# One tower layer on one core: GELUs of the second group behind the sines of the first, its last projections between the chunks, means as extra columns

## The reference, cut to what matters

```
h   = silu(layernorm([atom_embed[x], (rel_dist masked @ neighbor_embed[x]) * w_rd] @ w1 + b1)) @ w2 + b2
x1  = layernorm(h)
# attention without a softmax, by phases
content, values, key_ph = x1 @ mc_w, x1 @ ve_w, tanh(x1 @ cpe_w) * PI
ao      = gelu([x1, pp] @ hop_w1 + b) @ hop_w2 + b       # 4 heads x (32 phases + 1 width)
center, width = tanh(ao[:32]) * PI, sigmoid(ao[32]) * 2 + 0.1
gate    = sigmoid(gelu(x1 @ sg_w1 + b) @ sg_w2 + b)
ctx     = cumsum(x1 @ kce_w + b) / pos
st_ph   = tanh(gelu([x1, ctx] @ ksk_w1 + b) @ ksk_w2 + b) * PI
# causal sums over cos/sin of position, centre (5 shifts, weighted), key and stored phases
comb    = mh_out(content, center, width) + kv_ret(values * gate, key_ph, st_ph)
h       = h + x1 + layernorm(comb) @ out_w + out_b
x2      = layernorm(h)
h       = h + sum over the top 2 of 8 experts of (gelu(x2 @ W1[e] + b1[e]) @ W2[e] + b2[e])
```

## Time and profile before

| | |
|---|---|
| median of 3 runs | 169.94 us (169.46 to 170.4) |
| profiled execution, its own time | 169.19 us |
| its span | 167.4 us |
| busy in the span: PE / PEld | 149.0 us / 88.4 us |
| DVE / ACT / POOL | 116.6 / 81.8 / 8.8 us |
| spin products (L590) | 24.5 us of PE |
| ten of them from 58.60 | 2.32 us |
| chain that ended last | PE 54%, DVE 32%, ACT 6%, issue 6% |
| table loads on ACT | 1.28 us each |

### The profile page before, as it was taken

The page is one execution under the profiler, slowest core; times in us unless marked ns, Lnnn a source line. Parts: engine busy times, 40 slices in busy tenths (PEclk is TensorE's granted clock), DMA queues, the critical chain, the costliest instruction groups (busy, mean ns, idle before and its releaser), DMA issues.

```text
span 167.4 us, 2358 instructions
## 1 busy us (share of the span) xinstructions
PE 149.0 (89%) x806; PEld 88.4 (53%) x812; DVE 116.6 (70%) x344; ACT 81.8 (49%) x137; POOL 8.8 (5%) x38
## 2 busy tenths in 40 slices
PE   5899999999999988649699997786999999899991
PEld 1382565537693336429586752463665764553530
DVE  6999879975798989499859899993434788031202
ACT  3001151469389637962970232897224366545721
POOL 5403100140000000000000000000000000000000
PEclk9999999999999999956858999999999999999999
DMA  4899950300000000000000000000000000002011
GB/s 119 321 427 427 417 205 6 125 0 0 0 4 0 0 0 2 0 2 0 0 4 0 0 4 0 0 2 0 0 4 0 0 4 0 0 0 63 0 31 31
DMA packets 3778, 9.21 MB, mean 55 GB/s; under 512 B 2356, under 2 KB 2484, under 8 KB 3256
## 3 DMA queue, kind: packets, MB, share of 16 engines
q1 hardware_dynamic: 3768, 9.08, 14.6%
HBM read 8.55 MB, written 0.52 MB: 54 GB/s over the span
## 4 chain that ended last, share of the span: by engine, by line
PE 54%; DVE 32%; ACT 6%; issue 6%; POOL 0%; DVEq 0%; POOLq 0%; ACTq 0%
PE bank L960 9%; PE bank L944 6%; PE bank L646 5%; PE bank L945 4%; PE bank L624 3%; PE bank L807 2%; DVE invpos L1035 2%; PE bank L637 2%; DVE q_sc L1295 2%; DVE q_sc L1288 2%; PE bank L712 1%; PE bank L812 1%; PE bank L603 1%; PE bank L676 1%; DVE dist_sb L1274 1%
## 5 line engine op out<-in xcount | busy, mean ns | idle before, releaser
L590 PE MATMUL bank<-spin 128*128 128x512 bf16 x92 | 24.5, 398 | 5.2 <-POOL spin L328 2.0
L574 ACT ACTIVATE hid<-bank 128x512 f32<-128x512 f32 x32 | 17.9, 602 | 21.5 <-PE bank L945 21.4
L590 PEld LDWEIGHTS bank<-spin 128*128 128x128 bf16 x98 | 9.2, 104 | 15.8 <-issue 2.7
L960 PE MATMUL bank<-hid,ffn_sb 128*64 128x512 f32 x64 | 16.4, 612 | 0.0
L944 PE MATMUL bank<-xp,w1hi 128*128 128x512 f32 x32 | 14.6, 455 | 0.9 <-ACT xp L554 0.9
L1406 DVE TENSOR_TENSOR h<-bank,h 128x256 f32<-128x256 f32 (+1 forms) x5 | 1.8, 367 | 18.6 <-PE bank L971 12.8
L1313 DVE TENSOR_TENSOR dist_sb<-bank,fold_sb 128x256 f32<-128x256 f32 x16 | 6.0, 419 | 10.4 <-PE bank L812 9.8
L945 PE MATMUL bank<-xp,w1lo 128*128 128x512 f32 x32 | 12.6, 395 | 0.0
L944 PEld LDWEIGHTS bank<-xp,w1hi 128*128 128x128 f32 x32 | 6.0, 188 | 7.9 <-ACT hid L574 3.6
L646 PE MATMUL bank<-dist_sb,neigh 128*64 128x512 f32 x32 | 9.3, 699 | 0.0
L1085 DVE TENSOR_TENSOR dist_sb<-dist_sb,mask_in 128x1024 f32<-128x1024 f32 x8 | 9.2, 1218 | 0.0
(11 more groups left out here) (270 smaller groups left out, 318.3 us busy)
## 6 DMA issues: line engine op xcount, KB each, us to landing
dist_sb<-in_dist SPq DMA_DIRECT2D x4, 1024.0 KB, 11.2
mask_in<-in_mask SPq DMA_DIRECT2D x2, 512.0 KB, 8.1
fold_sb<-in_folded SPq DMA_DIRECT2D x1, 998.0 KB, 11.0
ffn_sb<-in_ffn SPq DMA_DIRECT2D x1, 816.0 KB, 17.4
late_sb<-in_late SPq DMA_DIRECT2D x1, 728.5 KB, 15.9
mask_in<-in_mrows SPq DMA_DIRECT2D x1, 512.0 KB, 3.1
out<-h SPq DMA_DIRECT2D x8, 64.0 KB, 1.7
early_sb<-in_early SPq DMA_DIRECT2D x1, 167.0 KB, 2.4
```

Source lines behind the costliest of these rows:

```text
L574: nc.scalar.activation(hid[:, at % HB], bank[hid_bank[at % 3]][:, :], ACT.Gelu).then_inc(S["hid_set"], 1)
L590: nc.tensor.matmul(bank[i][:, :], spin[:, 0:P], spin[:, :], start=True, stop=True)
L960: mm = nc.tensor.matmul(bank[2][j * D:(j + 1) * D, :], K["e_w2"][:, (e + j) * D:(e + j + 1) * D], hid[:, (at + j) % HB], start=False, stop ...
```

## The change

1. **Means as columns.** `w2_mean` and `out_mean` become the last two columns of `w2_ext` and `outw_ext` [128, 130]. The products write chunks 0, 1 to bank 5 and chunks 2, 3 to bank 7; the separate mean products go; VectorE reads rows and means in two halves.
2. **Position part first.** The product of the position phases opens the hop accumulation, ahead of the wait for x_t, in place of three spins.
3. **GELUs.** For group 1 ScalarE's hop, gate and ksk GELUs are one step, P1(2), which `ORDER` puts behind Q0(6), the first group's sines. For that TensorE makes group 1's storage product (into bank 6) and last joints in P1(2) too, with spins and waits between.
4. **Order.** Group 1's P(3), P(4), P(5) lie between the first group's chunk steps C(2) to C(5); Q1(4), Q1(5) come behind X0(2), and Q1(6) behind X0(4). From C1(1) on the order is the old one.
5. `weight_parts` is moved one step later and its expert half becomes `expert_parts`, after the third mask step. More spins in C0(1), C0(2) and X0(4).

```diff
+        w2_ext = sb("w2_ext", [P, PM])                       # PM = P + NH_
+        w2c_bd, w2_mean = w2_ext[:, 0:P], w2_ext[:, P:PM]
+        outw_ext = sb("outw_ext", [P, PM])
+        ksk_bank = (2, 6)
+        def with_mean(n):
+            return bank[5 + 2 * n][:, 0:2 * PM].rearrange("p (c d) -> p c d", d=PM)
...
@@ ScalarE, project @@
                 nc.scalar.activation(sg_g[:, :], bank[2][0:2 * SGH, :], ACT.Gelu,
                                      bias=K["sg_b1"]).then_inc(S["sg_set"], 1)
-                yield
+                if g == 0:
+                    yield
                 act.wait_ge(S["ksk_mm"], g + 1)
...
+                nc.scalar.activation(ksk_g[:, :], bank[ksk_bank[g]][:, :], ACT.Gelu,
                                      bias=ksk_bias[:, :]).then_inc(S["ksk_set"], 1)
+                if g:
+                    yield
@@ TensorE, token @@
                 for c in range(NC):
-                    mm = nc.tensor.matmul(bank[5][:, c * P:(c + 1) * P], f_t[:, c * P:(c + 1) * P], w2c_bd[:, :],
+                    mm = nc.tensor.matmul(with_mean(c // 2)[:, c % 2], f_t[:, c * P:(c + 1) * P], w2_ext[:, :],
                                           start=True, stop=True)
...
-                    mm = nc.tensor.matmul(bank[7][:, c * NH_:(c + 1) * NH_], f_t[:, c * P:(c + 1) * P], w2_mean[:, :],
-                                          start=True, stop=True)
@@ TensorE, project @@
-                spin_products(3, 2)
+                if g:
+                    pe.wait_ge(S["st_set"], g)
+                nc.tensor.matmul(bank[1][:, :], K["hop1p"], K["pp_T"], start=True, stop=False)
                 pe.wait_ge(S["xt_set"], g + 1)
-                nc.tensor.matmul(bank[1][:, :], K["hop1x_bd"], x_t[:, :], start=True, stop=False)
-                nc.tensor.matmul(bank[1][:, :], K["hop1p"], K["pp_T"], start=False, stop=True).then_inc(S["hop_mm"], 1)
+                nc.tensor.matmul(bank[1][:, :], K["hop1x_bd"], x_t[:, :], start=False, stop=True).then_inc(S["hop_mm"], 1)
...
                 joint(0, 3)
                 joint(1, 0)
-                yield
                 if g:
                     pe.wait_ge(S["h1_norm"], NG)
-                    spin_products(4, 6)
-                    pe.wait_ge(S["k_feat"], 2)
-                    spin_products(6, 6)
-                    pe.wait_ge(S["at_arg"], 1)
-                    spin_products(6, 6)
+                    storage()
+                    pe.wait_ge(S["h_mean_set"], NG)
+                    spin_products(4, 7)
+                    pe.wait_ge(S["phi_set"], 1)
+                    spin_products(5, 7)
+                    pe.wait_ge(S["th_sum"], 2)
+                    spin_products(5, 7)
+                    pe.wait_ge(S["th_set"], 2)
+                    spin_products(3, 7)
+                    last_joints()
+                    spin_products(3, 7)
+                    pe.wait_ge(S["cos_set"], 1)
+                    spin_products(5, 7)
+                    pe.wait_ge(S["cos_set"], 2)
+                    spin_products(5, 7)
+                yield
@@ TensorE, chunks @@
+                if g == 0:
+                    pe.wait_ge(S["h_mean_set"], NG)
+                    spin_products(4, 2)
+                    pe.wait_ge(S["kph_abs_set"], 1)
+                    spin_products(5, 2)
+                    pe.wait_ge(S["k_feat"], 1)
+                    spin_products(5, 2)
...
                 yield
+                if g == 0:
+                    pe.wait_ge(S["ksk_set"], NG)
+                    pe.wait_ge(S["q_cos"], 2)
+                    spin_products(5, 7)
                 pe.wait_ge(S["q_sum"], 2 * g + 2)
@@ TensorE, chunks, step 8 @@
-                    mm = nc.tensor.matmul(bank[5][:, c * P:(c + 1) * P], cc_t[:, c * P:(c + 1) * P], outw_g[:, :],
+                    mm = nc.tensor.matmul(with_mean(c // 2)[:, c % 2], cc_t[:, c * P:(c + 1) * P], outw_ext[:, :],
                                           start=True, stop=True)
-                    mm = nc.tensor.matmul(bank[7][:, c * NH_:(c + 1) * NH_], cc_t[:, c * P:(c + 1) * P], out_mean[:, :],
@@ TensorE, experts, step 4 @@
                     spin_products(6, 2)
+                    pe.wait_ge(S["at_arg"], 2)
+                    spin_products(5, 2)
+                    pe.wait_ge(S["phi_set"], 2)
+                    spin_products(5, 2)
+                    pe.wait_ge(S["th_sum"], 4)
+                    spin_products(5, 2)
                     pe.wait_ge(S["first_best"], 1)
@@ VectorE, chunks, step 9 @@
-                link(nc.vector.tensor_tensor(v8(comb[:]), b3(5), bc(st_c[:, :], D), ALU.mult))
+                for n in range(2):
+                    dve.wait_ge(S["attn_mm"], 2 * g + n + 1)
+                    factor = st_c[:, 4 * n:4 * n + 4].rearrange("p (c f) -> p c f", f=NH_).unsqueeze(3).broadcast_to([P, 2, NH_, D])
+                    ins = nc.vector.tensor_tensor(comb[:, 2 * n:2 * n + 2], rows_of(n), factor, ALU.mult)
```

More of the change, by code:

```diff
@@ L284, in b3, with rows_of, means_of @@
             return bank[i][:, :].rearrange("p (t d) -> p t d", d=D)
+        def with_mean(n):
+            return bank[5 + 2 * n][:, 0:2 * PM].rearrange("p (c d) -> p c d", d=PM)
+        def rows_of(n):
+            return with_mean(n)[:, :, 0:P].rearrange("p c (f d) -> p c f d", d=D)
+        def means_of(n):
+            return with_mean(n)[:, :, P:PM]
         def pair(t, c):
@@ L713, in joint, with storage, last_joints @@
                                      stop=True).then_inc(S["vk_mm"], 1)
+                def storage():
+                    i = ksk_bank[g]
+                    nc.tensor.matmul(bank[i][:, :], K["ksk1x_bd"], x_t[:, :], start=True, stop=False)
+                    pe.wait_ge(S["cx_set"], g + 1)
+                    nc.tensor.matmul(bank[i][:, :], wk_bd[:, :], cx[:, :], start=False, stop=True).then_inc(S["ksk_mm"], 1)
+                def last_joints():
+                    for c, i in ((2, 3), (3, 0)):
+                        pe.wait_ge(S["vk_set"], NC * g + c - 1)
+                        joint(c, i)
                 joint(0, 3)
                 joint(1, 0)
-                yield
                 if g:
                     pe.wait_ge(S["h1_norm"], NG)
-                    spin_products(4, 6)
-                    pe.wait_ge(S["k_feat"], 2)
-                    spin_products(6, 6)
-                    pe.wait_ge(S["at_arg"], 1)
-                    spin_products(6, 6)
+                    storage()
[14 more added lines that the diff above has]
+                yield
                 pe.wait_ge(S["hop_set"], g + 1)
@@ L733, in project @@
                 mm.then_inc(S["z_mm"], 1)
-                nc.tensor.matmul(bank[2][:, :], K["ksk1x_bd"], x_t[:, :], start=True, stop=False)
-                pe.wait_ge(S["cx_set"], g + 1)
-                nc.tensor.matmul(bank[2][:, :], wk_bd[:, :], cx[:, :], start=False, stop=True).then_inc(S["ksk_mm"], 1)
-                for c, i in ((2, 3), (3, 0)):
-                    pe.wait_ge(S["vk_set"], NC * g + c - 1)
-                    joint(c, i)
+                if g == 0:
+                    storage()
+                    last_joints()
                 yield
@@ L868, in chunks @@
                 for c in range(NC):
-                    mm = nc.tensor.matmul(bank[5][:, c * P:(c + 1) * P], cc_t[:, c * P:(c + 1) * P], outw_g[:, :],
+                    mm = nc.tensor.matmul(with_mean(c // 2)[:, c % 2], cc_t[:, c * P:(c + 1) * P], outw_ext[:, :],
                                           start=True, stop=True)
-                mm.then_inc(S["attn_mm"], 1)
-                for c in range(NC):
-                    mm = nc.tensor.matmul(bank[7][:, c * NH_:(c + 1) * NH_], cc_t[:, c * P:(c + 1) * P], out_mean[:, :],
-                                          start=True, stop=True)
-                mm.then_inc(S["attn_mm"], 1)
+                    if c % 2:
+                        mm.then_inc(S["attn_mm"], 1)
                 yield
@@ L1168, in token @@
                 nc.vector.tensor_tensor(v8(x[:, g]), v8(h[:, g]), bc(st_r[:, :], D), ALU.mult).then_inc(S["x_set"], 1)
-                dve.wait_ge(S["h_mean_mm"], g + 1)
-                nc.vector.tensor_copy(h_mean[:, g], bank[7][:, 0:8]).then_inc(S["h_mean_set"], 1)
+                for n in range(2):
+                    ins = nc.vector.tensor_copy(h_mean[:, g, 4 * n:4 * n + 4].rearrange("p (c f) -> p c f", f=NH_), means_of(n))
+                ins.then_inc(S["h_mean_set"], 1)
                 yield
@@ L1335, in chunks @@
                     chunk_state(c - 1)
+                    if g == 0 and c == 2:
+                        expert_parts()
                     yield
```

48 lines of the change are left out of this document (27 added, 21 removed).

## The result

The changed kernel takes 171.26 us (median of 5 runs, 170.8 to 171.61) where the kernel before, on the same chip, takes 169.46 (168.53 to 170.4): ratio 1.010 [1.0052, 1.0147], 1.8 us slower. The profiled execution took 171.01 us, its span is 169.1 (before: 169.19 and 167.4).

The account below looks back on a forecast made before the run. Bounds: TensorE from 34.2 and from 115.3 us, VectorE from 88.0 to 114.3, ScalarE at the first group's sines. +3.4 - 0.7 = +2.7 gave 171.9 or 172.6, taken as 172.2; range 169.3 to 174.0.

Parts of the forecast that it names:

- the sum: Whole kernel: +3.4 up to the fourth hidden product and -0.7 in the tail make +2.7 us.
- the turn: From the scores to the experts: the kernel loses its lead, fourth hidden product at 118.7 against 115.28, +3.4 us.
- signs of being wrong: First expert GELU ending before 114, no fall in the clock row there, or scores starting before 103.
- Start, -0.7: First group's hop: position product first takes 0.8 us off the chain; with split additions the second group's chain arrives 0.7 earlier.
- Sines without table changes, -2.9: First group's sines: without the table load between them, VectorE ends the query features at 71.7 in place of 74.6.
- z late, 2.95 of idle: Behind the first group's query transposes: z is there at 75.85 and VectorE idles 2.95 us for it.
- The further waits: Between the first group's chunks: VectorE waits about 1.1 us for products and scores, and 0.35 for ScalarE's square.
- The rival "z not late": VectorE runs through without the 2.95 us, scores at 101.8, end about 167.5 with full clock, 170.0 without; chance 0.18.
- ScalarE's queue, +1.0: Behind the scores: sines run before the xp2 copies, first GELU out at 116.3, fourth hidden product 1.0 us later.
- with the clock +3.4: Ahead of the first hidden product: 3.95 us of TensorE idle drops the clock, making the delay +3.4 instead of +1.0.
- with the clock held: Rival at that gap: the same waits, all at 2.4 GHz, +0.3 us, about 170.0; chance 0.17.
- Tail, -0.7: Behind the second group's output product: mean products go, 0.81 us, less 0.1 for split additions ahead of h3.

Follow-up runs that it names:

- Experiment 5: The kernel before with only the position product of the hop put ahead of the wait for x_t, in place of three spins: 168.22 us against 169.36.
- experiment 4: The kernel before with only the means as two more columns; order, GELUs and hop product as before: 169.6 us against 169.36, ratio 0.9999.
- Experiment 7: The changed kernel with z products and output weights ahead of the first group's query transposes, projections pulled earlier: 169.83 us against 169.33 for the kernel before.
- experiment 2: The changed kernel, order kept, with 17 spin products behind the xp2 transposes where TensorE idled: 168.98 us against 169.36 for the kernel before.
- experiment 1: The changed kernel with only Q1(6), the second group's rounding and sines, put back ahead of VectorE's scores: 168.29 us against 169.36 for the kernel before.
- experiment 3: The kernel before with only Q1(6) moved behind X0(4), as the change has it: 172.69 us against 169.33, ratio 1.0216.

## Why the prediction was right, step by step

Direction, place and mechanism came out as forecast: 171.26 measured, 172.2 forecast. From the first transposes the profile shows +2.5, the sum said +2.7. That the two sums lie so close is in part luck: the turn was priced 0.3 too high and the tail 0.2 too favourable. None of the prediction's signs of being wrong appeared, though the scores, at 103.21, came within 0.2 us of theirs (a start before 103).

- *Start, -0.7.* The second group's x transposes follow the first group's by 18.31 us, 18.99 before: -0.68. Experiment 5 shows 0.81 in the chain and 0.78 at the end of the span, and experiment 4 the 0.14 that the split reads take back (19.13). Right.
- *Sines without table changes, -2.9.* The query features end at about 70.8, forecast 71.7; counted from the first x transposes they end 2.9 us earlier than before. Right. The loads cost 1.28 (67.73), and the next activation started at their end (69.02): the price by the rows held. The price of the Trainium skill, "ScalarE: Activation LUTs", section "What ACT_TABLE_LOAD costs", a load and a drain of 2.66 us together, did not.
- *z late, 2.95 of idle.* Measured 2.89. The further waits, forecast 1.45, came to 0.32, 0.42, 0.46 and 0.29, in sum 1.49. The scores, forecast at 104.5, started at 103.21; of the difference 0.85 is the earlier start of this execution.
- *The rival "z not late" fell* for the reason given: transposes and z are in one queue behind the GELUs. Experiment 7 made it true, and showed that the scores come 0.85 to 1.17 sooner and not the 2.7 of the rival, and the end 1.3 and not 2.2, since 1.38 of idle time returns 16 us later.
- *ScalarE's queue, +1.0, and with the clock +3.4.* The order is as forecast, the gap 4.13 against 3.95. At the first score product it came to +3.08; experiment 2 splits that into 0.67 for the late copies (forecast 1.0) and 2.41 for the clock (2.4). The forecast put all of it at the fourth hidden product, where 2.47 is reached; the rest fell on the slow products behind it. The first GELU was out at about 114.9 (114.30 and 0.6), 1.4 ahead of the forecast's 116.3; 0.85 of that is the start of the execution. One link was wrong without harm: with the clock held, the fourth hidden product was to wait for this GELU. In experiment 2 it follows the query transposes in TensorE's own queue, as it did before the change, and it is late because the first hidden products are. That Q1(6) behind the scores is the cause is shown twice, by taking it back (experiment 1) and by doing it alone (experiment 3). The Trainium skill, "TensorE: Matmul & The Clock Gate", section "HAM oscillation — how this bites in real kernels", has the array resume at half rate after a wait that is long enough. The granted 0.58 behind the gap agrees with it.
- *Tail, -0.7.* Right where it was placed, and 0.5 of it reaches the end. From the first score product of the same profile, the transposes of h come 0.66 us sooner than before and the end of the span 0.53. All seven profiled kernels with the means as columns end 49.5 to 49.6 us behind that product, the five without them 50.0 to 50.1. The saving is 0.89 where the products stood and shrinks behind it, a loss that I had not priced. That the edit alone changed no time (experiment 4) is not the tail's doing: its profile came to the first score product 0.47 late, 0.24 of it by a wait without a known releaser, and that loss the prediction did not have.
- *Size.* The time rose by 1.8, the profile by 2.5. What lies between, 0.7, is less than what the start moves one execution by (1.3 us over the twelve profiles), and no run here separates it further. The forecast of the time also stood on a median of before that came out 0.48 lower with the two later runs (169.94, then 169.46): against its own starting point it said +2.3, and +1.8 was measured.

The better order was on view in the rows: the earlier trace rows show ScalarE through with the sines when the copies came due. Keeping that, the rest of the change is a gain (0.9911).

## What to carry to other kernels

When a step moves in the written order, read the queue of each engine that it touches and ask which item behind it now waits: six activations of some 0.6 us each, behind the wrong wait, cost 3 us in two different kernels. A wait of 2 to 4 us on TensorE is priced by what runs behind it as well: the products that follow at 1.2 GHz cost more here than the gap, and spins in the gap gave 2.2 us back. That holds where TensorE is the bound behind the gap: in the first half, where VectorE was busy for 4.89 of the 5.10 us behind the gap, spins in a gap of 3.8 us left the profile's scores where they were, and the clock fell at the next gap. A saving on a bound engine can shrink behind its place (0.89 us at the output product, 0.66 at the transposes of h, 0.5 at the end), and idle time taken away in a queue shared by many steps comes back in part at the next step that it had covered.

## What the runs showed of the hardware

- A gap of 2.25 us of TensorE was followed by products at the 1.2 GHz level (experiment 1, 1.92 us for eight transposes); I had priced only those near 4 us. The length of the last gap alone does not tell it: in the kernel before the granted clock was 0.99 from 78.6 to 82.0 and 0.51 from 82.0 to 86.0, and the longest idle time of TensorE in either stretch was 0.94 us. Once fallen, the level showed in the rows from 73.5 to 78.6 and, after, from 112.64 to some 118.5, where the output products (L1003, 1.08) are at full pace again.
- Reading a bank in two halves of 256 in place of one of 512 took 0.76 us against 0.69, and the pair for the means 0.26 up to the next operation against 0.19: 0.14 in all up to the scores.
- 130 columns per matmul against 128 are not visible: eight took 1.14 us in either form, and the next product started 0.89 or 0.90 behind the first of them (0.97 before).
